# Relative-position attention on one core: diagonal score blocks joined to their rows, score banks shared by neighbouring rows, a ring of six probability buffers, and context products in three groups a head

## What is computed

```python
xh = xn.reshape(b, s, H, Dh)
q, k, v = xh @ Wq + bq, xh @ Wk + bk, xh @ Wv + bv
content   = einsum('bqhd,bkhd->bhqk', q + u_bias, k)
pos_score = _rel_shift(einsum('bqhd,khd->bhqk', q + v_bias, p))
attn = softmax((content + pos_score) / sqrt(e), axis=-1)
ctx  = einsum('bhqk,bkhd->bqhd', attn, v)
```

## Time and profile before

| | |
|---|---|
| Time, median of 3 runs | 1631.8 us (1630.96 to 1640.66) |
| Profiled execution | 1633.4 us, of which span 1631.7 us |
| Mean granted TensorE clock | 0.958 |
| PE, DVE, ACT, POOL busy, share of the span | 92%, 83%, 67%, 65% |
| A steady batch of eight heads | 139.3 us |

### The profile page before, as it was taken

The page is one execution under the profiler, slowest core; times in us unless marked ns, Lnnn a source line. Parts: engine busy times, 40 slices in busy tenths (PEclk is TensorE's granted clock), DMA queues, the critical chain, the costliest instruction groups (busy, mean ns, idle before and its releaser), DMA issues. The chain is left out here.

```text
span 1631.7 us, 49008 instructions
## 1 busy us (share of the span) xinstructions
PE 1506.8 (92%) x12235; PEld 1163.5 (71%) x12236; DVE 1350.0 (83%) x5147; ACT 1094.5 (67%) x2267; POOL 1059.1 (65%) x2019
## 2 busy tenths in 40 slices
PE   4799999999999999999999999999940899999997
PEld 2566777777776777777767677766530899999997
DVE  5689899899989989998898998888533788888886
ACT  3167777777777777777777777766710677777775
POOL 3177667667766766776776676656754376666666
PEclk8599999999999999999999999999965899999999
DMA  6836445544643653553464455333153244443443
GB/s 165 234 100 178 125 133 156 145 119 110 197 112 107 178 153 96 145 167 101 126 179 134 122 158 158 106 87 81 37 164 99 46 59 54 54 57 52 54 57 46
DMA packets 129820, 189.79 MB, mean 116 GB/s; under 512 B 20184, under 2 KB 93272, under 8 KB 129616
## 3 DMA queue, kind: packets, MB, share of 16 engines
q1 hardware_dynamic: 104048, 167.23, 37.8%
q0 software_dynamic: 25568, 20.14, 8.2%
HBM read 104.04 MB, written 69.96 MB: 107 GB/s over the span
## 5 line engine op out<-in xcount | busy, mean ns | idle before, releaser
L1122 DVE CUSTOM_DVE_ANT_0 junk<-pA,lmask 128x512 bf16<-128x512 f32 x1024 | 669.2, 683 | 78.8 <-PE pA L685 64.3
L1017 ACT ACTIVATE prob<-pB 128x512 f32<-128x512 f32 x384 | 230.1, 599 | 178.3 <-PE pB L704 96.8
L1653 POOL DMA_INDIRECT out<-yb,dst x142 | 229.5, 1616 | 131.6 <-ACT yb L1731 78.5
L706 PE MATMUL pB<-QL,K 97*128 97x512 f32 (+3 forms) x768 | 284.1, 371 | 1.4 <-ACT upper_diag L1017 1.2
L683 PE MATMUL pA<-K,QL 96*128 96x512 f32 (+3 forms) x768 | 272.7, 356 | 12.6 <-DMA K<-split_operands 11.1
L704 PE MATMUL pB<-QU,K 97*128 97x512 f32 (+3 forms) x640 | 265.3, 415 | 3.0 <-ACT prob L1017 2.2
L1019 ACT ACTIVATE prob<-pB 128x512 f32<-128x512 f32 x384 | 228.2, 594 | 12.8 <-PE pB L706 2.5
L685 PE MATMUL pA<-K,QU 96*128 96x512 f32 (+3 forms) x640 | 224.9, 352 | 1.8 <-DVE acc L1122 0.6
L722 PE MATMUL pC<-prob,vext 128*17 128x256 f32 x3088 | 217.0, 384 | 0.3 <-POOL prob L597 0.3
L597 POOL TENSOR_TENSOR prob<-prob,upper_diag 128x128 f32<-128x128 f32 x384 | 185.6, 483 | 32.1
L704 PEld LDWEIGHTS pB<-QU,K 97*128 97x128 f32 x640 | 121.1, 189 | 107.9 <-issue 62.6
(11 more groups left out here) (308 smaller groups left out, 3477.0 us busy)
## 6 DMA issues: line engine op xcount, KB each, us to landing
QL<-split_operands SPq DMA_DIRECT2D x64, 256.0 KB
QU<-split_operands SPq DMA_DIRECT2D x64, 256.0 KB
K<-split_operands SPq DMA_DIRECT2D x64, 256.0 KB
xg<-routed_rows SPq DMA_DIRECT2D x75, 132.0 KB
split_operands<-c_h SPq DMA_DIRECT2D x32, 256.0 KB, 5.6
split_operands<-c_l SPq DMA_DIRECT2D x32, 256.0 KB, 5.9
QL<-split_operands SPq DMA_DIRECT2D x64, 128.0 KB
QU<-split_operands SPq DMA_DIRECT2D x64, 128.0 KB
```

Source lines behind the costliest of these rows:

```text
L706: mm = pe.matmul(pB[:, q0 + up:q0 + HALF], K[0:r, s, k], QL[0:r, s, q0 + up:q0 + HALF], start=True, stop=True)
L1017: act.activation(p[:, 0:HALF], pB[:, 0:HALF], ACT.Exp, scale=SCALE).then_inc(p_exp, 1)
L1122: v.tensor_tensor_reduce(out, src[:, :], lmask[:, at:at + HALF], 1.0, -3.0e38, ALU.add, ALU.max, acc[:, s, qb, n % 2:n % 2 + 1]).then_inc( ...
L1653: po.indirect_dma_start(dram["out"], bass.IndirectOffsetOnAxis(dst[k][:, a:a + 1], 0), yb[k][:, a, :], None, compute_op=ALU.add).then_inc( ...
```

## The change

Blocks are now listed by tables. Within a half of 4 x 4 blocks ("own"), a bank holds the rest of one row from its diagonal block on in one form and the row before it up to and with its diagonal block in the other: 4, 3 + 1, 2 + 2, 1 + 3 and 4 blocks. So each diagonal block is part of a wider matmul in both forms, and two neighbouring rows share a bank. The far half of each row stays a bank of one matmul. Both passes have 18 banks a head, as before, of 24 matmuls in place of 30. In the second pass a key block's probabilities now lie in two units' buffers, the lower diagonal block in unit kb and the upper one in unit kb + 1, so the buffers form a ring of 6 over units and `upper_diag` is gone. POOL does, per unit, the mask of an upper diagonal block with the corner element beside it, the sum, and the mask of the next lower one. DVE still has 24 reductions a head, 12 of 512 columns and 12 of 128, 256 or 384, with a mask in bf16 for both forms. The context products run in three groups: key blocks 5 to 7 at unit 1 of the next head, 0 and 1 at unit 4, 2 to 4 at unit 6; none at unit 8.

```diff
-RING = 4
-LATE = 2
+RING = 6
+LATE = 3
+HELD = 4
-        upper_diag = [sb(f"upper_diag{i}", [P, S]) for i in range(2)]
-        PAIRS_AT = {1: (-1, 6), 4: (0, 0), 6: (0, 2), 8: (0, 4)}
+        GROUPS_AT = {1: (-1, 5, 3), 4: (0, 0, 2), 6: (0, 2, 3)}
...
+        def first_banks():
+            own, far = {}, {}
+            for at in (0, OWN):
+                own[at] = [[(UPPER, at, at, 4)], *([(UPPER, at + r, at + r, 4 - r), (LOWER, at + r - 1, at, r)] for r in (1, 2, 3)), [(LOWER, at + 3, at, 4)]]
...
+            return (a[0], a[1], far[0], far[1], a[2], far[2], a[3], far[3], a[4], d[0], d[1], far[4], far[5], far[6], d[2], d[3], far[7], d[4])
+        def second_banks():
...
+            return ((a[0], far[0]), (a[1], far[1]), (a[2], far[2]), (a[3], far[3]), (a[4], d[0]), (d[1], far[4]), (d[2], far[5]), (d[3], far[6]), (d[4], far[7]))
+        def kept_at(h, u):
+            return prob[(h * S2U + u) % RING]
...
-            for i in range(1, RING):
+            for i in range(2, RING):
                 po.memset(prob[i][:, :], 1.0).then_inc(set_pool, 1)
...
-                        if u == 0:
-                            p = upper_diag[h % 2][:, :].rearrange("p (n q) -> p n q", q=P)
-                            po.affine_select(out=p, in_=p, ...).then_inc(diag_masked, 1)
+                        if u > 0:
+                            kb = u - 1
+                            p = upper_row[:, at - edge:at + P]
+                            po.affine_select(out=p, in_=p, ...).then_inc(upper_masked, 1)
+                            po.tensor_tensor(p_upper if kb % 2 else p_lower, p_lower, p_upper, ALU.add).then_inc(p_mask, 1)
+                        if u < NB:
+                            p = lower[:, at:at + P]
                             po.affine_select(out=p, in_=p, ...).then_inc(lower_masked, 1)
...
-                        if u in PAIRS_AT:
+                        if u in GROUPS_AT:
+                            back, from_kb, many = GROUPS_AT[u]
+                            for kb in range(from_kb, from_kb + many):
+                                context(b, h + back, kb)
...
-                        if u > 0:
-                            act.wait_ge(pv_done, b * (H * NB) + h * NB + u)
-                        p = prob[(u - 1) % RING] if u > 0 else upper_diag[h % 2]
+                        if u < RING:
+                            act.wait_ge(pv_done, b * (H * NB) + h * NB + min(u + S2U - RING, NB - 1) + 1 - NB + HELD + LATE)
+                        else:
+                            act.wait_ge(pv_done, b * (H * NB) + h * NB + u - RING + 1 + HELD + LATE)
+                        p = kept_at(h, u)
```

## The result

The change made the kernel slightly slower: 1641.1 us (median; 1638.1 to 1645.8) against 1632.5 for the kernel before on the same chip, ratio 1.0042 with a 95% interval of 1.0026 to 1.0059. The forecast was 1586 in a range of 1562 to 1612. The profiled execution after has a span of 1636.4 us at a mean granted clock of 0.953 (before 1631.7 and 0.958). Runs in a slower state of the chip, of which two fell among those used here (1852 and 2059 us), are left out of every comparison.

What follows compares the result with a forecast made beforehand. TensorE was taken to bound the kernel, VectorE 9% behind. Seven batches × 5.8 = 40.6 us and 5.7 in the last, less prologue and tail costs, gave −45.5: 1586 us against the median, range 1562 to 1612.

Steps and rivals of the forecast that it cites:

- Joined blocks: Diagonal blocks inside wider matmuls on TensorE: each of four banks a head gives back about 0.17 to 0.2 us.
- The sum: TensorE's unit-by-unit changes added up: −1.2 us a head, −9.6 a batch, bringing 139.26 us to 129.7 by TensorE alone.
- Units 8, 1, 4 and 6: Unit 8 falls from 2.26 to 1.25 us, 1 rises from 2.20 to 2.59, 4 falls to 2.17, 6 rises to 2.6.
- I take 1.25 for units 8 and 0: Units 8 and 0 shrink to 1.25 us, near the 1.19 of units without other work on TensorE.
- what is late next: VectorE alone needs about 130.8 us a batch, TensorE 129.7; mutual losses of 2.7 make a batch 133.5.
- VectorE as a sum: VectorE's 126.80 us of busy time a batch do not shrink; with its gaps it needs about 130.8.
- 24 gaps: VectorE runs dry while context groups of three products bring no new bank: 2 to 6 us a batch, 4 taken.
- two engines in lockstep over three banks: TensorE and VectorE, nearly equally long, cost each other 2 to 4 us a batch, 2.7 taken; the fourth head already lost 0.49.
- The last batch: First passes in six heads only, little other VectorE work: 0.95 × 6 = 5.7 us gained, nothing in its last two heads.
- slower rival: Unit 6's key block 4 product waits for GpSimd's sum beyond 0.9 us of slack; 1.1 a head gives 1653. Chance 0.04.
- nearly free: A scatter (1.10 us) or position product in unit 4 leaves GpSimd 0.5 to 1 us backlog, against 0.9 free.
- new waits eat most of it: Uncovered VectorE gaps, late unit 5 sums, or only the regrouping counting leave near 1602 to 1613 us; chance 0.19.

Runs made afterwards that it cites:

- joined kernel: The changed kernel with the four context groups of before, so only the diagonal blocks are joined: 1599.0 us, ratio 0.9787 to the kernel before.
- VectorE and ScalarE light: The changed kernel with VectorE's one-piece bank reductions cut to 256 columns and ScalarE's unit 8 evacuations and splits to 64: 1603.5 us, ratio 0.9795.
- covering placement: The changed kernel with its three context groups at units 1, 5 and 8 instead of 1, 4 and 6: 1634.4 us, ratio 1.0004.
- narrow products: Joined blocks, four groups, one group's context products 16 columns wide a strip instead of 256: at unit 8 1607.4 us, at unit 4 1603.5 us.
- pieces moved: The changed kernel with unit 0's small pieces one unit later, behind unit 1's context group: 1662.9 to 1670.9 us, ratio 1.0202.
- cut at unit 4: Joined blocks, four groups, unit 4's context products 16 columns wide a strip instead of 256: 1603.5 us, ratio 0.9827.

## Why the prediction was wrong

**Joined blocks**: right in mechanism, over-sized. The sum had 0.4 for unit 0, 0.24 for unit 4, part of unit 6 and 0.1 elsewhere; alone they gave 0.25, 0.19 and 0.25, and units 2, 3, 5 and 7 took 0.17 back: −0.55 a head, −34 us.

The Trainium skill ("TensorE: Matmul & The Clock Gate", "Back-to-back issue gap") would, by its isolated gap, have had this edit save nothing; the same section says that this formula counts too little at N = 128 in a stream of weight loads and matmuls. The joined kernel's ratio of 0.9787 and the 0.44 against 0.24 us of the earlier trace rows do not agree with the isolated gap.

**Units 8, 1, 4 and 6**: right. 1.25 taken, 1.30 measured; 2.59 and 2.65; 2.18 and 2.23; 2.56 and 2.61 (means over heads). The loop over the exponential is unit 8's floor.

**The step that failed** is "I take 1.25 for units 8 and 0", with what stood behind it, "what is late next". For unit 0 the mean was to fall by 0.4 to 1.42 and came to 2.04: 0.62 a head, 5.0 a batch. The floor was read from the last heads, which have no first pass and no pieces. A unit with pieces ends when the piece's operand is there, and in unit 0 of heads 0, 1, 5 and 7 that comes from VectorE or ScalarE, queued behind unit 8's banks. In heads 3 and 4, where no such wait is listed, unit 0 is 0.4 above the joined kernel's and lost nearly all of that when ScalarE's evacuations in unit 8 were cut. Units 2, 3, 5 and 7 are 0.27 a head over the sum (2.2 a batch); the other four are 0.24 (1.9). In all TensorE's 129.7 us of a batch became 138.7: 9.0 lost where 3.8 were counted, and 5.2 by seven batches is 36 us of the miss. The span was to change by −45.5 and changed by +4.7: of these 50 us the seven batches hold 40 (some 4.5 of them in the two disturbed by a lower clock) and the last one 10.8.

**VectorE as a sum** was the wrong measure. Its busy time did not change (126.17 of a batch, forecast 126 to 127), nor does it bind on average: 91% of a batch, where 95% were forecast. The loss that I looked for at the groups of three is there: in front of the first bank behind them, in units 2 and 7, VectorE stands 6.5 us a batch, 1.4 in the joined kernel (I had 4 for 24 gaps, of which only 16 are behind groups of three). VectorE's timeline in head 2, unit 7:

```profile
687.71 0.42 DVE L1161 CUSTOM_DVE_ANT_0 junk<-pA,mask 128x256 bf16<-128x256 f32 x1 [0.46 <-PE pA L723]
```

In heads 2 and 3, which VectorE fills, such gaps of 0.46 and 0.44 us more than in the joined kernel go with heads that are 0.45 and 0.43 longer: 0.9 us a batch. But TensorE's waits came where I had not looked, and where there was no group: in unit 0 VectorE runs two banks and a 1.2 us product behind TensorE, and the small pieces, and in head 1 ScalarE's queue, ask for its results at fixed places. These waits come without any group of three as well, once unit 8 is short. Also, the 0.49 us of the fourth head that I read as two engines in lockstep over three banks were for 0.37 a piece's wait, the line `rows_r` in the list of the kernel before: the mechanism of unit 0 stood in that row. The other engines' totals (GpSimd 105.10, under the 109 of the sum) told nothing of this.

**The last batch** was to gain 5.7 us and lost 5.1. In head 0 a context group of unit 1 stops over 1 us with no release shown, which the joined kernel has too; unit 6 waits for GpSimd, the slower rival's mechanism, once and long:

```profile
1071.09 0.63 PE L756 MATMUL pC<-prob,vext 128*17 128x256 f32 x8 [2.08 <-POOL prob L633]
```

TensorE stood 2.08 us for the sum of key block 4, where 0.9 us of slack were counted. GpSimd's timeline there:

```profile
1069.13 0.99 POOL L572 DMA_INDIRECT routed_rows<-sent,sent_to  x1 [1.84 <-ACT b_all L1055]
...
1070.59 0.45 POOL L633 TENSOR_TENSOR prob<-prob 128x128 f32<-128x128 f32 x1
```

A scatter stood ahead of that block's select and sum, and itself began 1.84 us after the work before it. ScalarE's exponential that the profile names was over at 1068.42, 0.7 before the scatter; what held it in between the trace does not name. The price for a scatter was put at "nearly free", and in the steady batches it cost nothing that shows. Behind this stop TensorE's clock was 0.57 and 0.50 from 1071.2 to 1080.0 (1.00 in that head before the change), so more than the 2.08 us was lost by it.

**The rivals.** The result lies beyond "new waits eat most of it", mostly by waits in a place that I had not named. The regrouping is not merely worth nothing, it loses 25 us (alone) to 42 (on top of the joining, 1641.1 to 1599.0; the two profiled executions differ by 34). Of those 34, the seven batches hold 24.8 and the last one's first six heads 6.6.

**What stays open**: why units 8 and 0 together give back so little. With VectorE and ScalarE light they fall by 0.58 a head for products that had taken 0.98, while units 1 and 6 take 0.48 and 0.55 for products that start 0.44 behind the one before; that, and the last batch's first six heads (105.8 us against 102.8), is 23 of the 28 us that three groups lose there. At the covering placement unit 5 alone took 1.59 more. ScalarE's and GpSimd's shares were not measured apart, and ScalarE's wait for `vsh` ahead of unit 0's exponential was not moved. Nor was it tried to give the pieces' VectorE work an earlier place in its queue.

## What to carry to other kernels

A long unit on the bounding engine may be the cover of another engine's chain: before moving its work away, read from that engine's timeline how far behind it is at that point, and which operand the next small pieces take from it, and look for waits on it in the queues of third engines. Take a unit's floor from a unit with the same side work, not from a bare one. When a change has two parts, time each alone: here one gave −34 us and the other hid it. When a time does not move, look at the granted clock of the stages before saying that the work was hidden.

## What the runs showed of the hardware

TensorE's granted clock fell to half right after short stops. In the kernel after, the windows from batch 3's head 0 into its head 1 (from 512.40 on) are:

```profile
498.00:512.00 14.00, 14.00 (x116) 9.15 (x115) 13.52 (x51) 9.90 (x21) 11.28 (x24) 1.00 0.41 108
512.00:515.40 3.40, 2.22 (x11) 1.21 (x9) 3.40 (x12) 2.14 (x6) 2.84 (x5) 1.00 0.57 146
515.40:520.20 4.80, 4.79 (x29) 2.21 (x29) 2.52 (x11) 2.13 (x4) 2.92 (x6) 0.50 1.01 263
```

TensorE was busy for all of the first 14 us, idle for 1.18 of the next 3.40, and then ran 4.8 us at 1.2 GHz. Head 1 took 21.47 us at a mean clock of 0.84, 2.9 more than the same head of batch 4. The same stop (the wait for `vsh`) is there in each of the seven batches before the last, the drop in batches 0 and 3 only; what decides was not found. Head 7 of batch 6 took 19.27 us at a clock of 0.91, 17.70 at 1.00 in batch 4. Three kernels had the lowest mean clocks: 0.941 and 0.937 with narrow products, 0.944 with the pieces moved, against 0.955 for the joined one. In two of them TensorE's work had turned into waiting, and the clock took back what a batch had saved: with the cut at unit 4 a batch at a clock of 1.00 is 2.5 us shorter than the joined one, batches 2 to 6, each with one head at 0.76 or 0.77, are 1.4 to 1.9 us longer.
